# Layer 1 edge visits: look-ups of group g+2 amid the sums of group g, a third buffer of transposed one-hots, a fifth sum bank, and 96 semaphore increments per group on SyncE

## What is computed

```python
h = (x @ W).reshape(n, NHEAD, OUT_FEATS)
h_l = (a_l * h).sum(-1)
h_r = (a_r * h).sum(-1)
e = h_l[row] + h_r[col]
e = jnp.where(e > 0, e, ALPHA * e)
m = jax.ops.segment_max(e, row, num_segments=n)
ex = jnp.exp(e - m[row])
denom = jax.ops.segment_sum(ex, row, num_segments=n)
att = ex / (denom[row] + 1e-16)
msg = att[:, :, None] * h[col]
out = jax.ops.segment_sum(msg, row, num_segments=n)
```

## Time and profile before

| | |
|---|---|
| median of 3 runs | 4150.6 us (4141.25 to 4151.45) |
| the profiled execution | 4167.99 us, of which its span is 4166.3 us |
| busy: PE, DVE, ACT, POOL | 67%, 60%, 38%, 53% of the span |
| the stage of the layer 1 visits | about 2108 us to 3420 us of the span |

### The profile page before, as it was taken

The page is one execution under the profiler, slowest core; times in us unless marked ns, Lnnn a source line. Parts: engine busy times, 40 slices in busy tenths (PEclk is TensorE's granted clock), DMA queues, the critical chain, the costliest instruction groups (busy, mean ns, idle before and its releaser), DMA issues. The chain is left out here.

```text
span 4166.3 us, 48622 instructions
## 1 busy us (share of the span) xinstructions
PE 2771.2 (67%) x12850; PEld 2189.0 (53%) x12850; DVE 2489.0 (60%) x5847; ACT 1566.9 (38%) x5077; POOL 2220.9 (53%) x2162
## 2 busy tenths in 40 slices
PE   5466776567677754824666676666667665699983
PEld 4233344355555543713555465555555545599972
DVE  5345998677777786434545555555555567544438
ACT  6663000067787831113422232233233223333334
POOL 0366777766666602555256666666666641265530
PEclk9678888788898965967867767677776675799985
DMA  5232333323333313632234444444444464122234
GB/s 146 86 88 83 89 87 89 88 85 90 90 93 91 95 57 91 152 76 71 78 89 114 109 114 113 109 115 109 113 113 112 111 112 150 62 72 70 71 96 143
DMA packets 220767, 408.50 MB, mean 98 GB/s; under 512 B 51598, under 2 KB 134545, under 8 KB 220371
## 3 DMA queue, kind: packets, MB, share of 16 engines
q0 software_dynamic: 102192, 279.12, 25.2%
q1 hardware_dynamic: 118308, 126.27, 10.2%
HBM read 342.96 MB, written 62.28 MB: 97 GB/s over the span
## 5 line engine op out<-in xcount | busy, mean ns | idle before, releaser
L534 POOL DMA_INDIRECT arena<-h_table,arena x1712 | 1751.6, 1023 | 1016.0 <-issue 482.5
L548 DVE TENSOR_TENSOR arena<-arena,ps 128x260 f32 (+1 forms) x1712 | 719.6, 420 | 905.0 <-remote 407.0
L2199 PE MATMUL ps<-arena 128*128 128x260 f32 x1760 | 667.1, 538 | 415.9 <-DVE arena L548 282.6
L2199 PEld LDWEIGHTS ps<-arena 128*128 128x128 f32 x1760 | 441.5, 268 | 591.3 <-issue 457.0
L1216 PE MATMUL ps<-arena 128*128 128x256 f32 x1664 | 556.7, 451 | 252.5 <-DVE arena L548 133.1
L1216 PEld LDWEIGHTS ps<-arena 128*128 128x128 f32 x1664 | 328.1, 222 | 410.2 <-issue 238.2
L717 ACT ACTIVATE arena<-arena 128x112 f16<-128x112 f16 x1568 | 446.5, 375 | 88.1 <-DVE arena L983 77.6
L2066 ACT ACTIVATE ps<-arena 128x32 f32<-128x32 f32 x110 | 22.1, 201 | 953.8 <-DVE arena L2122 784.6
L884 DVE TENSOR_SCALAR arena<-arena 128x128 f32<-128x128 f32 x832 | 290.4, 350 | 0.4
L2181 PEld LDWEIGHTS ps<-arena 128*128 128x128 f32 x1760 | 273.2, 236 | 16.6 <-issue 4.5
L2132 DVE TENSOR_TENSOR arena<-arena,ps 128x1024 f32<-128x1024 f32 x220 | 267.2, 1215 | 0.0
(11 more groups left out here) (520 smaller groups left out, 4289.0 us busy)
## 6 DMA issues: line engine op xcount, KB each, us to landing
arena<-visit_lanes SPq DMA_DIRECT2D x110, 256.0 KB
arena<-h_table,arena POOLq DMA_INDIRECT x1712
arena<-in_L_ffn_w SPq DMA_DIRECT2D x32, 512.0 KB, 7.4
xn_table<-arena SPq DMA_DIRECT2D x14, 896.0 KB, 4.0
slot_out<-arena SPq DMA_DIRECT2D x21, 512.0 KB
arena<-y_rows SPq DMA_DIRECT2D x12, 896.0 KB, 9.5
h_table<-arena SPq DMA_DIRECT2D x7, 924.0 KB
h_table<-arena SPq DMA_DIRECT2D x7, 896.0 KB, 4.2
```

The lines of the kernel that those rows point to most:

```text
L534: pool.indirect_dma_start(slot[:, 0:width], None, table, bass.IndirectOffsetOnAxis(ap=idx, axis=0)).then_inc(done, 16)
L548: dve.tensor_tensor(to, to, bank(b, width), ALU.add).then_inc(gnn_add, 1)
L2199: pe.matmul(bank(sum_bank(g * U + u), ACC_W), hot[:, g % 3, u, :], rows[r][:, u, 0:ACC_W], start=True, stop=True).then_inc(gnn_ps, 1)
```

## The change

It makes five edits in the stage of the layer 1 visits.

1. `look_up(g + 2)` now stands in the middle of the sums of g (ahead of u = 4) in place of `look_up(g + 1)` ahead of them; the look-ups of groups 0 and 1 stand ahead of the loop.
2. `hot_t` has a third buffer; DVE makes the one-hots one group earlier (`hot_lanes(g + 3)` in `attend(g, 4)`), and waits for the look-up of three groups back instead of two.
3. The sums go round five banks (4, 5, 6, 7, 0) in place of four (4, 5, 6, 0).
4. Bank 7 is no longer free for the copy of iota, so ACT reads iota from SBUF for all groups.
5. SP, behind each load of `lanes`, increments the new semaphore `beat` 96 times. Nobody waits for it.

```diff
@@ -454,7 +454,7 @@
         edges_ready, hot_done, gnn_ps, gnn_add = (sem(n) for n in (
             "edges_ready", "hot_done", "gnn_ps", "gnn_add"))
 
-        GNN0_BANKS, GNN1_BANKS = 8, 4
+        GNN0_BANKS, GNN1_BANKS = 8, 5
         V0_BANKS = 4
         RING = 2 * U
 
@@ -2000,6 +2000,8 @@
 
         lanes = [take(U * P // 2).bitcast(BF16) for _ in range(2)]
         hot_t = [take(U * P) for _ in range(2)]
+        hot_t.append(arena[:, XNT + (R - 1) * SLOT_W:XNT + (R - 1) * SLOT_W + U * P])
+        assert XNT + (R - 1) * SLOT_W + U * P <= ACC
         lc = take(BUCKETS * 2 * GH)
         r_max = take(GH)
         score = take(U * GH).rearrange("p (u h) -> p u h", u=U)
@@ -2008,7 +2010,6 @@
         hot = take(3 * U * P).rearrange("p (b u n) -> p b u n", b=3, u=U)
         r_rows = arena[:, place["at"] - GH * P:place["at"]]
         assert place["at"] <= arena_words - KD * P - SLOT_W
-        lanes_ps = bank(7, P)
         ex_ps = bank(1, U * GH).rearrange("p (u h) -> p u h", u=U)
         lc3 = lc.rearrange("p (t w) -> p t w", w=2 * GH)
         rl3 = rl_all.rearrange("p (t w) -> p t w", w=2 * GH)
@@ -2021,10 +2022,11 @@
         (rm_done, rm_ps, lc_done, hots_done, hott_done, look_ps, score_done, ex_done, msg_done, den_in) = (
             sem(n) for n in "rm_done rm_ps lc_done hots_done hott_done look_ps score_done ex_done msg_done den_in".split())
         lane_in = [sem(f"lane{b}_in") for b in range(2)]
+        beat, BEATS = sem("beat"), 96
         A = Steps(nc.scalar, sem("act_step"))
 
         def sum_bank(n):
-            return (4, 5, 6, 0)[n % GNN1_BANKS]
+            return (4, 5, 6, 7, 0)[n % GNN1_BANKS]
 
         with nc.Block() as block:
             @block.sync
@@ -2034,6 +2036,8 @@
                         sp.wait_ge(hott_done, g - 1)
                     sp.dma_start(lanes[g % 2], visit_lanes[g * U * P:(g + 1) * U * P].partition_broadcast(P)
                                  ).then_inc(lane_in[g % 2], 16)
+                    for _ in range(BEATS):
+                        sp.sem_inc(beat, 1)
 
             @block.gpsimd
             def _(pool):
@@ -2049,12 +2053,12 @@
 
             @block.scalar
             def _(act):
-                def apart(g, of):
+                def apart(g):
                     if g >= 3:
                         act.wait_ge(gnn_ps, (g - 2) * U + (SUMS_BEFORE + R * U))
                     for u in range(U):
                         n = g * U + u
-                        last = act.activation(hot[:, g % 3, u, :], of, ACT.Abs, bias=v_loc[:, n:n + 1], scale=-1.0)
+                        last = act.activation(hot[:, g % 3, u, :], iota, ACT.Abs, bias=v_loc[:, n:n + 1], scale=-1.0)
                     A.add(last)
 
                 def match(g):
@@ -2069,7 +2073,7 @@
                 act.copy(acc.rearrange("p (a b) -> p a b", b=ZERO_W), zeros[:, 0:ZERO_W].unsqueeze(1).to_broadcast(
                     [P, BUCKETS * ACC_W // ZERO_W, ZERO_W])).then_inc(edges_ready, 1)
                 for g in range(2):
-                    apart(g, iota)
+                    apart(g)
                     A.settle()
                     match(g)
                 weigh(0, 0)
@@ -2077,7 +2081,7 @@
                     if g + 1 < GROUPS1:
                         weigh(g + 1, (g + 1) % R)
                     if g + 2 < GROUPS1:
-                        apart(g + 2, lanes_ps)
+                        apart(g + 2)
                         A.settle()
                         match(g + 2)
 
@@ -2101,9 +2105,9 @@
 
                 def hot_lanes(g):
                     dve.wait_ge(lane_in[g % 2], g // 2 * 16 + 16)
-                    if g >= 2:
-                        dve.wait_ge(look_ps, g - 1)
-                    dve.tensor_scalar(hot_t[g % 2], lanes[g % 2], lane, None, ALU.is_equal).then_inc(hott_done, 1)
+                    if g >= 3:
+                        dve.wait_ge(look_ps, g - 2)
+                    dve.tensor_scalar(hot_t[g % 3], lanes[g % 2], lane, None, ALU.is_equal).then_inc(hott_done, 1)
 
                 def attend(g, u):
 
@@ -2122,8 +2126,8 @@
                         dve.scalar_tensor_tensor(score, look[:, :, GH:], OTHER, score, ALU.add, ALU.subtract
                                                  ).then_inc(score_done, 1)
                     elif u == 4:
-                        if g + 2 < GROUPS1:
-                            hot_lanes(g + 2)
+                        if g + 3 < GROUPS1:
+                            hot_lanes(g + 3)
                     elif u in MSG_AT:
                         dve.wait_ge(ex_done, g + 1)
                         q = MSG_AT.index(u) * HALF_U
@@ -2140,8 +2144,8 @@
                     a = xres[:, c * B * D:(c + 1) * B * D]
                     dve.tensor_tensor(a, a, half(4 * (c % 2), 0, B * D), ALU.add).then_inc(mx_add, 1)
                 dve.wait_ge(mx_add, LOOPS)
-                V.then(dve.tensor_copy(lanes_ps, iota))
                 dve.wait_ge(edges_ready, 2)
+                hot_lanes(2)
                 for u in range(U):
                     attend(0, u)
                 for g in range(GROUPS1):
@@ -2178,21 +2182,21 @@
 
                     pe.wait_ge(hott_done, g + 1)
                     for u in range(U):
-                        last = pe.matmul(bank(2 + g % 2, LW, u * LW), hot_t[g % 2][:, u * P:(u + 1) * P],
+                        last = pe.matmul(bank(2 + g % 2, LW, u * LW), hot_t[g % 3][:, u * P:(u + 1) * P],
                                          lc[:, ds(tiles[u] * LW, LW)], start=True, stop=True)
                     last.then_inc(look_ps, 1)
 
-                look_up(0, load_tiles(pe, 0))
-                tiles = load_tiles(pe, U)
+                for g in range(2):
+                    look_up(g, load_tiles(pe, g * U))
                 for g in range(GROUPS1):
                     r = g % R
-                    if g + 1 < GROUPS1:
-                        look_up(g + 1, tiles)
                     if g + 2 < GROUPS1:
                         tiles = load_tiles(pe, (g + 2) * U)
                     pe.wait_ge(hots_done, g + 1)
                     pe.wait_ge(den_in, g + 1)
                     for u in range(U):
+                        if u == HALF_U and g + 2 < GROUPS1:
+                            look_up(g + 2, tiles)
                         if u % HALF_U == 0:
                             pe.wait_ge(msg_done, g * 2 + (u // HALF_U + 1))
                         pe.wait_ge(gnn_add, g * U + (ADDS_BEFORE + u + 1))
```

## The result

The change made the kernel slower: 4371.6 us, median of 4 runs (4366.2 to 4374.0), against 4145.9 us of the kernel before in the same session (4 runs, 4133.0 to 4151.5). The ratio is 1.0549, interval 1.0526 to 1.0572. The forecast was 4001 us.

The account below looks back on a forecast made before the run. The prediction took late signals in the layer 1 visits as the bound. From the profiled 4168.0 us it took 150 us for the increments and nothing for the other edits, then 17.4 us to the median: 4001 us, range 3940 to 4185.

Parts of the forecast that it names:

- What bounds the kernel: Layer 1 visits: late signals between POOL, PE and DVE, not work, make groups 12.05 us; at most 211.4 us to regain.
- The increments bring signals on time: Layer 1 visits: SP's 96 increments end POOL's "remote" waits and a sixth of its PE waits, 150 us; chance 0.40.
- the bounds for the cost of one increment: SP's queue in layer 1 visits: 0.069 to 0.11 us each, so 6.6 to 10.6 us a group.
- rival C: Layer 1 visits: above 0.121 us an increment, SP's round delays lanes loads and sets the pace; 4244 us at 0.13; chance 0.08.
- Rival B: Layer 1 visits: increments delay signals between PE and DVE, 97 us at most, half on the path, 4200 us; chance 0.14.
- estimate by the Trainium skill: SP's increments serialize ahead of PE's at 26.3 ns each: 2.5 us a group, 278 us in all, 4429 us.
- Fifth bank: Layer 1 sums: PE runs one sum further ahead of DVE, shortening DVE's waits for PE by 0 to 106 us.
- second case: Layer 1 visits: increments do nothing, bank and order alone gain 40 us (0 to 106), 4110 us; chance 0.25.
- Look-ups amid the sums: PE in layer 1 visits: look-ups ahead of the fifth sum put at nothing; 204 us without cover by an existing wait.
- iota from SBUF: ACT in layer 1 visits: 387 instead of 381 ns, 8 times a group, under ACT's idle time: nothing.
- The signs to look for: Layer 1 waits and gather times named beforehand to tell the cases apart, such as SP's load ending DVE's waits at hot_lanes.
- the sign for the likeliest case: DVE's add has almost no "remote" waits, POOL's waits fall from 211 to about 60 us, gathers 33 to 880 take about 1127.

Follow-up runs that it names:

- e2: The kernel before with SP's 96 increments a group added and nothing else, on a prompt chip: 1.0007 against 3687.5 us.
- e13: The changed kernel with 32 increments a group in place of 96, on a late chip: 1.0115 against the kernel before at 4171.8 us.
- e14: The changed kernel with four banks and no increments, moved look-ups and third buffer kept, on a late chip: 1.0110 against the kernel before at 4171.8 us.
- e16: The kernel before, but from group 4 ACT issues the lanes loads and SP makes 72 increments a group, waiting for nobody; late chip: 1.0260 against 4136.4 us.
- e17: The kernel before with ACT issuing the lanes loads from group 4 and SP making no increments from there, on a late chip: 1.0006 against 4136.4 us.

## Why the prediction was wrong

**What bounds the kernel: right.** The stage was read as held by late signals, with POOL able to do a group in 10.05 us. On the prompt chips, where no signal is late, the stage runs at 10.3 us a group with almost nothing but "issue" ahead of the gathers, close to these 10.05 us. The kernel before is 463 us (11%) shorter there, more than the 211 us that the prediction ascribed to late signals in this stage; another 192 us of it lie in layer 0's visits, as shown next.

**"The increments bring signals on time": refuted.** This was the likeliest case (0.40) and the whole gain of 150 us. It rested on layer 0's waits being short, and that reading left out half: it took the waits that are put down to PE. The same view of the kernel before, 700 to 1450 us, has further down:

```profile
DVE arena L548 <- remote: 35.5, 11, 14.8
...
POOL arena L534 <- remote: 21.6, 8, 4.9
```

So signals are late in layer 0 as well, up to 14.8 us. Its gathers run from 143.6 to 1472.0 us in the kernel before, and from 144.3 to 1280.4 us in e2, on a prompt chip with the same layer 0: 192 us less. Layer 0 was no example of busy engines that keep signals on time. 32 increments do nothing (e13 against e14), and 72 that nothing stands behind cost 42 us.

**The step that failed: the bounds for the cost of one increment, 0.069 and 0.11 us.** They decided that SP's increments are covered by SP's waits. The bounds were taken from a register instruction of DVE and from the gap between two adds. Undisturbed, an increment takes 0.059 us, below the lower bound. In this kernel on a late chip it takes 0.147 us, above the upper one, and rival C's condition, over 0.121 us, was met. C was put at 0.08 because "it is above my upper bound of 0.11". Its mechanism is what happened, point by point: the loads of `lanes` late, groups as long as SP's round. Its price at 0.147 us, by its own formula (96 x 0.147 + 0.4 = 14.5 us, less 12.05, x 110), would have been 270 us; measured were 209 in the stage. The range, 3940 to 4185, left "all of C" out. The increments were to gain 150 us and cost 209. The prediction had itself found that semaphore signals are held up for microseconds in this stage, and then priced SP's semaphore work by rows that hold no such delay.

**Rival B, the increments get in the way: real but small.** 42 us in e16 against e17, at 72 increments, which is inside its 97 us at most. What it costs in the change itself, beside SP's round, was not measured apart. The prediction's estimate by the Trainium skill (TensorE: Matmul & The Clock Gate, "The cost: per-tile semaphore tail"), 4429 us, comes nearer to 4371.6 than the forecast, by luck. The Trainium skill's rule, a fixed time for each increment that adds up, is not what the runs show when it is carried over to SP: on a prompt chip 96 and 160 increments cost 0.1%, and 240 cost 14%.

**Fifth bank, 0 to 106 us, 40 with the order: nothing,** 0.9995. The prediction said that sums done and unseen do not shorten a long stop, and in its second case still gave 40 us for the short waits and the order. The forecast of 4001 us did not use them.

**Look-ups amid the sums, "nothing": a loss of 1%** (1.0089 to 1.0110, some 43 us). The prediction named what stands behind them, and 204 us as the price without cover, but asked only for PE's time. What moved was the place of the stop.

**iota from SBUF: right.** 387 ns, 262.5 us in all, no idle time ahead.

**The signs to look for** did their work. SP's load ends DVE's waits at `hot_lanes`, and the group lasts as long as SP's round; for this the prediction had named C or the upper bound of an increment. "Remote" fell to 188.8 us without any gain, so the sign for the likeliest case was met in part by a slower kernel.

## What to carry to other kernels

A queue that waits most of its time is free only up to its round: write down the round (count x price + issue) against the shortest group, and if a factor of 1.4 in the price, here 0.11 to 0.15 us, turns the sign, give that case a large chance. When a trace shows signals that arrive late, every semaphore instruction in that stretch has two prices, and the upper bound is to be taken from the late ones. When something is moved past a place at which an engine stops, ask where the stop goes, not only what the moved instructions cost.

## What the runs showed that was not expected

- The same kernel takes 3684 to 3688 us on two chips and 4135 to 4172 us on three. In the stage of the visits that is 10.3 against 12.0 us a group, and "remote" waits of DVE of none against 349.5 us. Layer 0's gathers take 1136 against 1328 us.
- A bare increment of SP takes 0.059 us on a prompt chip. On a late one some 9% of them are held up for 0.6 to 0.8 us (978 of 10560), and PE's signals for up to 11 us; in e16, where SP does not pause, 1242 of 7920.
- The hold-ups end with the gathers and loads of the stage: in e16 0.220 us an increment until the last gather, 0.061 us behind it, on the same late chip.
- The long stop is tied to the burst of look-ups: moved half a group, it moved with them, in all seven kernels counted above.

Open stays what makes a chip late (one chip was measured in two sessions, the others in one, so that it is the chip and not the hour is not shown), why most hold-ups of SP's increments last about 0.7 us, and whether the lower clock in e16 is a cause of its stops.
